# Projection in two passes over batch 0, and the first head's stack over two rings

## The chip, the cores and the metric

The kernel runs on one core of a Trainium2 chip. A core has five engines that work side by side and meet at semaphores: TensorE (PE, matmuls into PSUM), VectorE (DVE), ScalarE (ACT), GpSimd (POOL) and SyncE (SP, which here only issues DMAs). DMAs can be issued from SP, ACT and POOL; each of the three has a ring of its own. The metric is the device time of one launch in microseconds (us), lower is better; several runs are taken and the median is given.

## The reference

One transformer block on x, two batches of 2048 rows of 256 features. What matters here is its first part:

```
h = layernorm(x) * (1 + ca) + sa
Q, K, V = h @ W.T + b + 2 * (h @ A.T @ B.T)       # for Wq, Wk, Wv: 256 x 256, rank 8
energy = Q K^T / 4                                # 16 heads of 16 features, per batch
out = softmax(energy) V                           # 2048 keys and 2048 queries per head
x = x + ga * (out @ Wo.T + ...)                   # then a gated feed-forward stage with 8 experts
```

sa, ca, ga come from a small matrix product with wmod. There are 2 x 16 = 32 (batch, head) pairs, called heads below. The output projection, the shared and the routed feed-forward stages follow; neither they nor the arithmetic of any step is touched.

## The kernel before

**Chunks.** x is cut into 8 chunks of 512 rows (NCH), 4 per batch (CPB). For each chunk DVE takes mean and variance (`moments`), ACT a square root (`root`), DVE normalizes (`normalize`), PE transposes the result into PSUM (`turn`), ACT applies scale and shift and writes hT (`modulate`). PE then makes four units `qk` (o = 0 and 1: the first and second 128 columns of Q; o = 2 and 3: the same of K) and two halves of V (`v`). Heads 0 to 7 of a batch live in units 0 and 2, so head 0 needs only those.

**Parts.** Each unit is cut into three bf16 parts whose sum is the fp32 value: ACT writes a copy and the first part (`take`), POOL the remainder, ACT the middle part (`middle`), POOL the last part; SP stores the three (384 KB) to DRAM as qk_parts (`store`). `take` and `middle` of ACT, and the two POOL steps, are in a written order, one engine instruction after the other.

**Stacks.** Before a head can run, `stack` reads its rows of Q and K parts back from DRAM into four tiles: q_high and k_high (64 KB and 128 KB a DMA, 8 DMAs), q_low and k_low. All 16 DMAs are issued by SP, in SP's order. There are three sets of tiles; the first three heads' stacks are issued during the projection. k_low also has rows of ones, and q_low has two rows that hold each query's negated maximum; those come from POOL tiles `mb` by four small DMAs of SP (`maxima`) once the head's maxima are known.

**Maxima.** For each head PE makes 32 pairs of matmuls k_high x q_high (`max_pair`, L847), and DVE takes a maximum of each (`reduce_pair`, L937). A pair needs two banks of a ring of three PSUM banks, so a pair directly behind a pair waits for DVE. Head 0's 32 pairs stand between the units of batch 1, as the table BESIDE says: 2 in chunk 4, then 8, 11 and 11. Behind them stand 12 pairs of head 1, mixed with four products for rowmod (L915), then the first scores of head 0 (`scores`, L870), which wait for head 0's two maximum rows through s_mrows. After that the 32 heads run in a steady rhythm.

**SP's order.** Loads; then per chunk of batch 0 the next x load and four stores; a wait for all of them; stack of head 0; chunk 4's stores; stack of head 1; four small late loads; chunk 5's stores; stack of head 2; three weight loads of 512 KB; the stores of chunks 6 and 7; then `maxima` of heads 0 and 1.

**Buffers.** Two tiles for x, two for the normalized x, two for hT, four for parts. POOL first fills rows of ones in three k_low tiles and clears three vs tiles, and then begins with the remainders.

Of the kernel before, what the change touches and what calls it, by code (L numbers as in the profile page):

```python
# [26 lines left out]
F32 = mybir.dt.float32  # L27
# [6 lines left out]
P = 128  # L34
# [29 lines left out]
STACK = 16 * 16  # L64
UQ = 2 * D // P
TAGS = 4
# [82 lines left out]
def block_kernel(nc, io, out):  # L149
    with ExitStack() as ctx:  # L150
# [72 lines left out]
        x_t = buffers("x_t", [P, TPC, D], F32, r)  # L223
        xn = buffers("xn", [P, TPC, D], F32, r)
        hT = buffers("hT", [P, HALF, CH], F32, r)
        qf = buffers("qf", [P, CH], F32, r, UQ)
        parts = buffers("parts", [P, 3, CH], BF16, r, UQ)
        stats = r("stats", [P, TPC, 6])
        mv = r("mv", [P, TPC, 2])
        std = r("std", [P, TPC])  # L230

        turned_sb = Region(nc, r.at, queries_at)("turned_sb", [KT, P])
# [3 lines left out]
        rest = buffers("rest", [P, CH], F32, r, UQ)  # L236
        loA = r("loA", [R, 4, D])
        loB = r("loB", [R, 4, D])

# [67 lines left out]
        s_wT = sem("s_wT")  # L307
        s_wmod = sem("s_wmod")
# [13 lines left out]
        s_x = [sem(f"s_xload{u}") for u in range(2)]  # L322
# [10 lines left out]
        s_parts = [sem(f"s_parts{o}") for o in range(UQ)]  # L333
# [3 lines left out]
        s_stack = [sem(f"s_stack{p}") for p in range(NB)]  # L337
        s_rows = sem("s_rows")
# [80 lines left out]
        def root(act, g):  # L419

            act.wait_ge(s_var, g + 1)
            act.activation(std[:], mv[:, :, 1], ACT.Sqrt, bias=eps[:, 0:1]).then_inc(s_std, 1)

        def moments(dve, step, g, u, nth):

            dve.wait_ge(s_x[u], 16 * (nth + 1))
            for t in range(TPC):
                st = dve.bn_stats(stats[:, t, :], x_t[u][:, t, :])
            step(st)
            hold(dve)  # L430
            for t in range(TPC):
                a = dve.bn_aggr(mv[:, t, :], stats[:, t, :])
            a.then_inc(s_var, 1)

        def normalize(dve, step, g, u):

            dve.wait_ge(s_std, g + 1)
            step(dve.reciprocal(std[:], std[:]))
            wait(dve, s_xn_free, g - 1)
            for t in range(TPC):  # L440
                a = dve.tensor_scalar(xn[u][:, t, :], x_t[u][:, t, :], mv[:, t, 0:1], std[:, t:t + 1],
                                      ALU.subtract, ALU.mult)
            a.then_inc(s_norm, 1)


        def setup_sync(sp):

            for dst, src in first_loads[:-1]:
                sp.dma_start(dst[:], src).then_inc(s_const, 16)
            sp.dma_start(wT[:], io["wT"]).then_inc(s_wT, 16)  # L450
            sp.dma_start(x_t[1][:], rows(io["x"], TPC, TPC)).then_inc(s_x[1], 16)
            dst, src = first_loads[-1]
            sp.dma_start(dst[:], src).then_inc(s_bv, 16)
            sp.wait_ge(s_norm, 1)
            sp.dma_start(x_t[0][:], rows(io["x"], 2 * TPC, TPC)).then_inc(s_x[0], 16)
            sp.dma_start(wmod[:, :, 512:], io["wmod"][:, :, 512:]).then_inc(s_wrow, 16)

        def setup_scalar(act):
            act.dma_start(x_t[0][:], rows(io["x"], 0, TPC)).then_inc(s_x[0], 16)
# [7 lines left out]
        def setup_tensor(pe):  # L467
            pe.wait_ge(s_const, 16 * (len(first_loads) - 1))
            for m in range(4):
# [3 lines left out]
            mm.then_inc(s_lora, 1)  # L473
            pe.wait_ge(s_wmod, 16)
# [5 lines left out]
            mm.then_inc(s_mcol, 1)  # L480

        def setup_vector(dve, step):
            step(dve.memset(eps[:], EPS))
# [3 lines left out]
            moments(dve, step, 0, 0, 0)  # L487
            normalize(dve, step, 0, 0)
# [4 lines left out]
            dve.wait_ge(s_lora, 1)  # L493
            for m in range(4):
                dst = wqkv[:, m] if m < 3 else woT[:]
                w = dve.scalar_tensor_tensor(dst.rearrange("p k d -> p (k d)"), ps[:, 4 + m, :], LORA_SCALE,
                                             wT[:, m].rearrange("p k d -> p (k d)"), ALU.mult, ALU.add)
            w.then_inc(s_weff, 1)
# [3 lines left out]
            moments(dve, step, 1, 1, 0)  # L502
            normalize(dve, step, 1, 1)
# [21 lines left out]
        def project_sync(sp):  # L525
            def load(g, u):
                sp.dma_start(x_t[u][:], rows(io["x"], g * TPC, TPC)).then_inc(s_x[u], 16)

            def store(g, b, j):

                for o in range(UQ):
                    half = o % 2
                    sp.wait_ge(s_qf_free, UQ + UQ * g + o + 1)
                    dst = qk_dram[o // 2].rearrange("s (b c) t -> c s b t", b=B)
                    sp.dma_start(dst[half * P:(half + 1) * P, :, bass.ds(b, 1), bass.ds(j * CH, CH)].squeeze(2),
                                 parts[o][:]).then_inc(s_parts[o], 16)
# [7 lines left out]
            sp.wait_ge(s_norm, NCH - 2)  # L544
            load(NCH - 1, 1)
            for o in range(UQ):
                sp.wait_ge(s_parts[o], 16 * (CPB + 1))
# [10 lines left out]
            for g in range(CPB + 2, NCH):  # L558
                store(g, 1, g % CPB)


        BESIDE = {CPB: 2, CPB + 1: 8, CPB + 2: 11, CPB + 3: PAIRS - 21}

        def units_beside(g):

            if g not in BESIDE:
                return iter(()), [0] * 7
            first = sum(n for c, n in BESIDE.items() if c < g)
            n = BESIDE[g]
            share = [0, 0, 0, 0, 0, 0, n] if g == CPB else [n * (i + 1) // 7 - n * i // 7 for i in range(7)]  # L570
            return iter(range(first, first + n)), share

        def project_tensor(pe):
            pe.sem_inc(s_v, 1)

            def turn(g, u):
                pe.wait_ge(s_norm, g + 1)
                wait(pe, s_hT, g)
                for k in range(HALF):
                    for t in range(TPC):  # L580
                        mm = pe.transpose(ps[:, k, t * P:(t + 1) * P], xn[u][:, t, k * P:(k + 1) * P], ident[:])
                mm.then_inc(s_xn_free, 1)

            def qk(g, u, o):
                pe.wait_ge(s_qbank_free, UQ * g + o + 1)
                for k in range(HALF):
                    mm = pe.matmul(ps[:, 2 + o % 2, :], wqkv[:, o // 2, k, (o % 2) * P:(o % 2 + 1) * P],  # L587
                                   hT[u][:, k, :], start=(k == 0), stop=(k == 1))
                mm.then_inc(s_unit, 1)

            def v(g, u, half):
# [1234 lines left out]
```

## Time and profile before

| what | us |
|---|---|
| median of 3 runs | 1972.77 |
| lowest and highest | 1971.50, 1974.07 |
| the profiled execution: its own time | 1975.94 |
| its span in the trace | 1974.1 |
| mean granted TensorE clock in it | 0.973 of full speed |

In the span PE is busy 1864.3 us (94%), DVE 1559.0, ACT 1245.7 and POOL 341.5. The span has three stretches. The projection and the lead into attention take the first 180 us, the 32 heads run from there to about 1480 us (some 40 us a head), and the rest is the output projection and the feed-forward part. A row of the timeline gives the start, the busy time of the group, engine, line, operation, tiles and count, and in brackets the idle time before it with what ended it. A fp32 matmul of the code is shown as two instructions in the trace. For an instruction that issues a DMA the time is that of the issue, not of the transfer.

### The profile page before, as it was taken

What the parts mean: (1) busy time and instruction counts of PE and PEld (TensorE: products, weight loads), DVE (VectorE), ACT (ScalarE), POOL (GpSimd) and SP (SyncE); (2) the same over time, 40 slices, a digit from 0 to 9 for tenths busy, and PEclk for the clock granted to TensorE, in tenths of its full rate; (3) what the DMA queues carried; (4) which work ended last, traced back from release to release, by engine and by line L of the source; (5) the groups of instructions that cost most, each with busy time, mean ns of one, the idle gap of its engine ahead of it and who ended that gap; (6) DMA issues with size and microseconds to landing.
All of it is one profiled execution on the core that took longest, in us unless ns stands there. A gap on an engine that the chain in (4) does not pass through costs nothing.

```text
span 1974.1 us, 34939 instructions
## 1 busy us (share of the span) xinstructions
PE 1864.3 (94%) x13114; PEld 770.4 (39%) x13115; DVE 1559.0 (79%) x2738; ACT 1245.7 (63%) x1426; POOL 341.5 (17%) x425
## 2 busy tenths in 40 slices
PE   7687999999999999999999999999984799999997
PEld 5332222222222222222222222222224556589996
DVE  5376999999999999999999999999816732245553
ACT  4534777777777777777777777777871221144442
POOL 6534200000000000000000000000015622223332
PEclk9898999999999999999999999999997799999998
DMA  4541111211112111111112111111047432322221
GB/s 160 167 149 37 42 41 39 61 57 43 41 46 68 46 41 41 58 59 42 41 48 65 49 38 39 57 56 41 7 143 227 164 102 91 117 81 73 72 72 48
DMA packets 89737, 141.52 MB, mean 72 GB/s; under 512 B 13104, under 2 KB 60208, under 8 KB 89472
## 3 DMA queue, kind: packets, MB, share of 16 engines
q1 hardware_dynamic: 74336, 102.01, 16.5%
q0 software_dynamic: 10240, 32.40, 5.0%
q10 hardware_dynamic: 5024, 5.24, 0.8%
q8 instruction: 91, 1.49, 0.3%
q14 instruction: 46, 0.38, 0.1%
HBM read 90.84 MB, written 48.51 MB: 71 GB/s over the span
## 4 chain that ended last, share of the span: by engine, by line
PE 81%; DVE 9%; DMA 3%; POOL 2%; issue 2%; ACT 1%; SPq 1%; POOLq 0%; DVEq 0%; ACTq 0%
PE ps L881 24%; PE ps L870 20%; PE ps L847 15%; PE ps L1560 7%; DVE mx L937 6%; PE ps L1111 5%; PE ps L1583 3%; PE ps L1445 3%; DMA l_in<-inverse_sums 2%; PE ps L587 1%; ACT prob L962 1%; POOL parts L727 1%; POOL rest L723 1%; PE ps L915 1%; PE ps L596 1%
## 5 line engine op out<-in xcount | busy, mean ns | idle before, releaser
L937 DVE TENSOR_REDUCE mx<-ps 128x1 f32<-128x512 f32 x2048 | 1273.3, 683 | 58.7 <-PE ps L847 55.5
L962 ACT ACTIVATE prob<-ps 128x1024 f32<-128x1024 f32 x1024 | 992.4, 1021 | 275.1 <-PE ps L870 272.6
L881 PE MATMUL ps<-prob,vs 128*32 128x512 f32 x4096 | 546.5, 605 | 0.7 <-ACT prob L962 0.7
L847 PE MATMUL ps<-k_high,q_high 64*128 64x512 bf16 x2048 | 400.8, 388 | 33.3 <-DMA k_low<-qk_parts 16.8
L870 PE MATMUL ps<-q_high,k_high 64*128 64x512 bf16 x2048 | 389.8, 377 | 3.3 <-ACT prob L962 2.2
L870 PE MATMUL ps<-q_low,k_low 34*128 34x512 bf16 x2048 | 390.0, 377 | 0.0
L847 PEld LDWEIGHTS ps<-k_high,q_high 64*128 64x128 bf16 x2048 | 99.1, 93 | 668.4 <-DVE mx L937 628.1
L1016 POOL CAST mb<-turned_sb 16x128 bf16<-16x128 f32 x32 | 8.9, 279 | 925.3 <-ACT turned_sb L975 896.9
L870 PEld LDWEIGHTS ps<-q_low,k_low 34*128 34x128 bf16 x2048 | 100.0, 94 | 116.9 <-issue 0.5
L870 PEld LDWEIGHTS ps<-q_high,k_high 64*128 64x128 bf16 x2048 | 101.5, 96 | 88.7 <-ACT prob L962 30.0
L881 PEld LDWEIGHTS ps<-prob,vs 128*32 128x32 f32 x4096 | 80.7, 108 | 118.7 <-issue 113.4
L1646 DVE TENSOR_TENSOR ehT<-esig,ps 128x512 f32<-128x512 f32 x39 | 26.8, 688 | 100.6 <-PE ps L1560 100.6
L1466 ACT ACTIVATE sgate<-ps 128x512 f32<-128x512 f32 x32 | 19.1, 597 | 121.6 <-PE ps L1111 121.6
L1607 ACT ACTIVATE esig<-ps 128x512 f32<-128x512 f32 x39 | 23.3, 597 | 113.4 <-PE ps L1560 113.4
L1319 DVE TENSOR_TENSOR hid<-sgate,ps 128x512 f32<-128x512 f32 x32 | 22.0, 687 | 76.5 <-ACT sgate L1466 76.5
L1560 PE MATMUL ps<-xsT,gate_w 128*128 128x128 f32 x624 | 76.1, 275 | 1.6 <-issue 1.0
L1560 PEld LDWEIGHTS ps<-xsT,gate_w 128*128 128x128 f32 x624 | 75.6, 192 | 3.9 <-issue 1.2
L1560 PE MATMUL ps<-xsT,up_w 128*128 128x128 f32 x624 | 76.1, 275 | 0.0
L1583 PE MATMUL ps<-rdT,ehT 128*128 x312 | 73.6, 379 | 0.0
L1560 PEld LDWEIGHTS ps<-xsT,up_w 128*128 128x128 f32 x624 | 72.8, 192 | 0.0
L1136 PE MATMUL ps<-woT,o_in 128*128 128x256 f32 x128 | 38.5, 469 | 33.2 <-DVE o_in L1187 33.2
L1111 PE MATMUL ps<-h2T,wgT 128*128 (+1 forms) x128 | 64.0, 625 | 4.4 <-DVE x L1197 4.1
(146 smaller groups left out, 1416.4 us busy)
## 6 DMA issues: line engine op xcount, KB each, us to landing
k_high<-qk_parts SPq DMA_DIRECT2D x128, 128.0 KB
qk_parts<-parts SPq DMA_DIRECT2D x32, 384.0 KB, 3.8
q_high<-qk_parts SPq DMA_DIRECT2D x128, 64.0 KB
k_low<-qk_parts SPq DMA_DIRECT2D x128, 64.0 KB
head_out<-head_out_sb SPq DMA_DIRECT2D x32, 256.0 KB, 10.8
sorted_in<-zero_row POOLq DMA_DIRECT2D x13, 390.0 KB, 7.3
xs<-sorted_in SPq DMA_DIRECT2D x39, 130.0 KB
q_low<-qk_parts SPq DMA_DIRECT2D x128, 32.0 KB
```

The source lines that it names most:

```text
L847: pe.matmul(ps[:, ring.bank((n, m, u)), :], q_high[p][mine, t * P:(t + 1) * P], k_high[p][mine, c * CH:(c + 1) * CH], start=True, stop=Tru ...
L870: mm = pe.matmul(ps[:, 2 * i + u, :], keys[mine, kt * P:(kt + 1) * P], queries[mine, i * CH:(i + 1) * CH], start=(n == 0), stop=(n == 1))
L881: mm = pe.matmul(ps[32 * j:32 * j + 32, 7, :], vs[buf(h)][:, kt, :], prob[:, kt % 2, j * CH:(j + 1) * CH], start=(kt == 0), stop=(kt == KT ...
L937: dve.tensor_reduce(mx[n % 2][:, at, c:c + 1], ps[:, ring.bank(what), :], AX.X, ALU.max).then_inc(s_ring, 1)
L962: act.activation(prob[:, kt % 2, :].rearrange("p (u c n) -> p u c n", u=2, c=2)[:, :, half, :], ps[:, 2 * half:2 * half + 2, :], ACT.Exp). ...
L1111: mm = pe.matmul(ps[:, at, :], w[:, k, fc * P:(fc + 1) * P], h2T[:, k, bass.ds(g * CH, CH)], start=(k == 0), stop=(k == 1))
L1136: mm = pe.matmul(ps[:, OUT_BANK[u] + t // 2, t % 2 * D:(t % 2 + 1) * D], o_in[u][:, k, t * P:(t + 1) * P], woT[:, k, :], start=(k == 0), s ...
L1445: mm = pe.matmul(ps[:, DOWN_BANK[u] + t // 2, t % 2 * D:(t % 2 + 1) * D], hid[u][:, fc, t * P:(t + 1) * P], wdT[:, fc, :], start=(fc == 0) ...
L1560: mm = pe.matmul(ps[:, bank, fc * P:(fc + 1) * P], w[u][:, c, fc * P:(fc + 1) * P], xsT[u][:, c, :], start=(c == 0), stop=(c == 1))
L1583: mm = pe.matmul(ps[:, 6 + u, 0:D], ehT[u][:, c, :], rdT[:, bass.ds(e, 1), c, :].squeeze(1), start=(c == 0), stop=(c == FC - 1))
L1607: act.activation(esig[u][:].rearrange("p c n -> p (c n)"), ps[:, egate_bank(k), :], ACT.Silu).then_inc(s_esig, 1)
L1646: dve.tensor_tensor(ehT[u][:].rearrange("p c n -> p (c n)"), esig[u][:].rearrange("p c n -> p (c n)"), ps[:, eup_bank(k), :], ALU.mult).th ...
```

## The change

Batch 0 is projected in two passes. The first makes units 0 and 2 of chunks 0 to 3 (eight units, EARLY), whose stores are all that head 0's stack needs. The second makes units 1 and 3 and V. hT of all four chunks stays in four tiles. The stack of head 0 goes out between the passes: its high tiles' first halves from SP, the second halves from POOL. Of the other DMAs of the stacks of heads 0 and 1, a few each stand between SP's stores; head 2's stack is issued behind the last store of chunk 7. `stack` now issues the eight high DMAs first, then six for the low tiles: q_low is read by one DMA per half in the place of two (64 KB, shaped 2 x 16 rows). The low tiles are counted with s_mrows.

x has eight tiles (four of them in the upper half of v_all, free until batch 1's V), all requested at once, normalized in place. The adapters and effective weights of Q and K are made before those of V and O. POOL's fills of ones wait for the second chunk's normalization, its clears of vs go behind the first pass. Parts have six tiles. Head 0's pairs stand 8 in chunk 3's second pass, in twos, and 6 in each chunk of batch 1, one behind each unit or half of V. The loops over chunks are written out.

**PE, from the adapters to the first pairs.** Before (the loop body over batch 0 stands once, and runs twice):

```order
L471 MATMUL ps<-loB,loA 128x256 x8
L478 MATMUL ps<-cS,wmod 128x2 x8
L581 MATMUL ps<-ident,xn_100 128x128 x8
...
L587 MATMUL ps<-hT_102,wqkv 128x512 x4
L596 MATMUL ps<-wqkv,hT_102 128x256 x4
L587 MATMUL ps<-hT_102,wqkv 128x512 x4
L596 MATMUL ps<-wqkv,hT_102 128x256 x4
L847 MATMUL ps<-k_high_66,q_high_81 128x512 x4
L581 MATMUL ps<-ident,xn_100 128x128 x8
```

After, from the first pass's end:

```order
L619 MATMUL ps<-hT_126,wqkv 128x512 x4
L619 MATMUL ps<-hT_127,wqkv 128x512 x4
L619 MATMUL ps<-hT_102,wqkv 128x512 x2
L628 MATMUL ps<-wqkv,hT_102 128x256 x4
...
L619 MATMUL ps<-hT_126,wqkv 128x512 x2
L628 MATMUL ps<-wqkv,hT_126 128x256 x4
L505 MATMUL ps<-ident,x_t_98 128x128 x8
L619 MATMUL ps<-hT_127,wqkv 128x512 x2
L909 MATMUL ps<-k_high_66,q_high_81 128x512 x4
```

The first pair stood behind the whole of chunk 4; it now stands behind the first pass, three chunks of the second pass (the dots), a transposition and one unit.

**SP, around the stack of head 2** (q_high_83 and k_high_68). Before, the stack stands behind chunk 5's stores, and the stores of chunks 6 and 7 behind it:

```order
L535 DMA qk_parts<-parts_111 128x3x512
L780 DMA q_high_83<-qk_parts 32x1x1024
L781 DMA k_high_68<-qk_parts 32x1x2048
...
L557 DMA wdT<-in_wdT 128x1024
L535 DMA qk_parts<-parts_108 128x3x512
...
L798 DMA q_low_84<-mb_73 1x8x128 x4
```

After:

```order
L581 DMA qk_parts<-parts_109 128x3x512
L829 DMA q_high_83<-qk_parts 32x1x1024
L830 DMA k_high_68<-qk_parts 32x1x2048
...
L610 DMA wdT<-in_wdT 128x1024
L858 DMA q_low_84<-mb_73 1x8x128 x4
```

The stack and the three weight loads now stand between the last store and the four DMAs for head 0's maximum rows (q_low from mb).

**POOL, at the end of the first pass,** after:

```order
L774 TENSOR_TENSOR parts_109<-rest_123,parts_109 128x512
L783 MEMSET vs_64 128x512
L784 MEMSET vs_64 128x16
...
L769 TENSOR_TENSOR rest_120<-qf_104,parts_110 128x512
L829 DMA q_high_81<-qk_parts 32x1x1024
L830 DMA k_high_66<-qk_parts 32x1x2048
L829 DMA q_high_81<-qk_parts 32x1x1024
L830 DMA k_high_66<-qk_parts 32x1x2048
L769 TENSOR_TENSOR rest_121<-qf_105,parts_111 128x512
```

POOL issued no DMA in the projection before; four now stand among its remainders, behind a wait for the first pass's stores.

The core of the diff:

```diff
 def project_sync(sp):
-    with sp.Fori(0, CPB // 2) as i:
-        for u in range(2):
-            g = 2 * i + u
-            sp.wait_ge(s_norm, g + 2)
-            load(g + 3, 1 - u)
-            store(g, 0, g)
...
-    stack(sp, (0, 0))
-    store(CPB, 1, 0)
-    stack(sp, (0, 1))
+    for g in range(CPB):
+        store(g, 0, 2)
+    parts_stored(sp, EARLY)
+    stack_high(sp, (0, 0), 0)
+    store(0, 1)
+    sp.dma_start(wmod[:, :, 512:], io["wmod"][:, :, 512:]).then_inc(s_wrow, 16)
+    store(0, 3)
+    sp.wait_ge(s_rows, 1)
+    stack_low(sp, (0, 0), 0)
+    store(1, 1)
+    stack_low(sp, (0, 0), 1)
+    store(1, 3)
+    stack_high(sp, (0, 1), 0)
...
-    store(CPB + 1, 1, 1)
+    for g in range(CPB, NCH):
+        store(g, *range(UQ))
     stack(sp, (0, 2))
     for dst, name in ((wgT, "wgT"), (wuT, "wuT"), (wdT, "wdT")):
         sp.dma_start(dst[:], io[name]).then_inc(s_shared, 16)
-    for g in range(CPB + 2, NCH):
-        store(g, 1, g % CPB)
 def project_tensor(pe):
+    pe.wait_ge(s_weff, 1)
+    for g in range(CPB):
+        if g + 1 < CPB:
+            turn_chunk(pe, g + 1)
+        pe.wait_ge(s_hT, g + 1)
+        qk(g, 0)
+        qk(g, 2)
+    pe.wait_ge(s_weff, 2)
+    for g in range(CPB - 1):
+        qk(g, 1)
+        v(g, 0)
+        qk(g, 3)
+        v(g, 1)
...
+            qk(g, 2 * i)
+            max_pair(pe, (0, 0), first)
+            qk(g, 2 * i + 1)
+            max_pair(pe, (0, 0), first + 1)
+            v(g, i)
+            max_pair(pe, (0, 0), first + 2)
 def project_gpsimd(pool, step):
+    pool.sem_inc(s_qf_free, UQ)
+    pool.wait_ge(s_norm, 2)
...
+    remainder(EARLY)
+    parts_stored(pool, EARLY)
+    stack_high(pool, (0, 0), 1, s_stack_first)
+    for n in range(EARLY + 1, UQ * NCH):
+        remainder(n)
+        last_part(n - 1)
+def stack_low(eng, h, u):
+    p, q_parts, k_parts = buf(h), qk_dram[0], qk_dram[1]
+    mine, first = slice(num(h) * DH, (num(h) + 1) * DH), u * HROWS
+    eng.dma_start(q_low[p][first:first + LROWS, :], q_parts[0:3:2, mine, u * HS:(u + 1) * HS]
+                  ).then_inc(s_mrows[p], 16)
```

## Rows read from the trace of the kernel before

**Rows 1.** PE's timeline, the start: start us, busy us, line, operation, tiles.

```profile
7.43 7.19 PE L471 MATMUL ps<-loB,loA 8*128 8x256 f32 x16 [7.43 <-DMA bqk_in<-in_bqk]
14.54 3.57 PE L478 MATMUL ps<-cS,wmod 128*128 128x2 f32 x16
17.98 1.95 PE L581 MATMUL ps<-ident,xn 128*128 128x128 f32 x8
...
24.21 4.09 PE L587 MATMUL ps<-hT,wqkv 128*128 128x512 f32 x8
```

**Rows 2.** A chunk of batch 0 on PE, and the wait behind batch 0.

```profile
35.03 1.04 PE L581 MATMUL ps<-ident,xn 128*128 128x128 f32 x8
35.90 3.60 PE L587 MATMUL ps<-hT,wqkv 128*128 128x512 f32 x8
39.34 1.89 PE L596 MATMUL ps<-wqkv,hT 128*128 128x256 f32 x8
41.07 3.60 PE L587 MATMUL ps<-hT,wqkv 128*128 128x512 f32 x8
...
96.82 0.61 PE L847 MATMUL ps<-k_high,q_high 64*128 64x512 bf16 x2 [16.84 <-DMA k_low<-qk_parts]
```

**Rows 3.** Batch 1 with head 0's pairs on PE, same view.

```profile
106.58 0.39 PE L847 MATMUL ps<-k_high,q_high 64*128 64x512 bf16 x2
...
108.83 0.39 PE L847 MATMUL ps<-k_high,q_high 64*128 64x512 bf16 x2
...
121.76 0.39 PE L847 MATMUL ps<-k_high,q_high 64*128 64x512 bf16 x2 [0.78 <-DVE mx L937]
...
127.69 0.39 PE L847 MATMUL ps<-k_high,q_high 64*128 64x512 bf16 x2 [1.06 <-DVE mx L937]
...
158.20 0.53 PE L847 MATMUL ps<-k_high,q_high 64*128 64x512 bf16 x2 [0.90 <-DVE mx L937]
```

**Rows 4.** The first scores of head 0 on PE, timeline of all engines.

```profile
180.71 0.38 PE L870 MATMUL ps<-q_high,k_high 64*128 64x512 bf16 x2
```

**Rows 5.** One chunk of batch 0 on ACT, from the timeline.

```profile
20.83 1.45 ACT L635 ACTIVATE hT<-ps,colmod 128x512 f32<-128x512 f32 x2
...
26.63 0.69 ACT L643 ACTIVATE qf<-ps,bqk 128x512 f32<-128x512 f32 x1 [0.63 <-PE ps L587]
...
29.50 0.62 ACT L650 CAST parts<-rest 128x512 bf16<-128x512 f32 x1
```

**Rows 6.** First normalization on DVE, beside POOL's fills.

```profile
9.39 4.81 DVE L441 TENSOR_SCALAR xn<-x_t,mv,std 128x256 f32<-128x256 f32 x4
```

**Rows 7.** POOL in the projection, from the timeline.

```profile
0.74 3.65 POOL L715 MEMSET k_low<- 2x2048 bf16 x2 [0.29 <-POOLq L1816]
...
30.81 1.15 POOL L727 TENSOR_TENSOR parts<-rest,parts 128x512 bf16<-128x512 f32 x1
```

**Rows 8.** SP in the projection, from the timeline: DMA issues.

```profile
76.57 0.78 SPq L780 DMA_DIRECT2D q_high<-qk_parts  x1
...
118.57 0.64 SPq L780 DMA_DIRECT2D q_high<-qk_parts  x1
...
130.76 0.43 SPq L557 DMA_DIRECT2D wdT<-in_wdT  x1
```

**Rows 9.** DMAs up to 150 us: KB each, median us to landing.

```profile
qk_parts<-parts SPq DMA_DIRECT2D x28, 384.0 KB, 3.9
...
k_high<-qk_parts SPq DMA_DIRECT2D x12, 128.0 KB
...
wdT<-in_wdT SPq DMA_DIRECT2D x1, 512.0 KB, 15.3
```

**Rows 10.** One us of attention; last three: granted clock, DMA share, GB/s.

```profile
1088.00:1089.00 1.00, 1.00 (x14) 0.29 (x12) 1.00 (x2) 0.67 (x1) 0.00 (x0) 1.00 0.13 51
```

**Rows 11.** A steady head's timeline: SP's first stack DMA, DVE's mneg.

```profile
1030.86 0.68 SPq L780 DMA_DIRECT2D q_high<-qk_parts  x1
...
1062.32 0.21 DVE L944 TENSOR_REDUCE mneg<-mx 128x16 f32<-128x64 f32 x1
```

More of the change, by code:

```diff
@@ L320, in block_kernel @@
         s_gates = sem("s_gates")
-        s_x = [sem(f"s_xload{u}") for u in range(2)]
+        s_x = [sem(f"s_xload{g}") for g in range(NCH)]
         s_var = sem("s_var")
@@ L465, in setup_scalar, with unit, adapt @@
             root(act, 1)
-        def setup_tensor(pe):
-            pe.wait_ge(s_const, 16 * (len(first_loads) - 1))
-            for m in range(4):
+        def unit(g, o):
+            return 2 * g + o // 2 if g < CPB and o % 2 == 0 else EARLY + 2 * g + o // 2 if g < CPB else UQ * g + o
+        def adapt(pe, first):
+            for m in range(first, first + 2):
                 for k in range(HALF):
@@ L492, in setup_vector @@
             dve.wait_ge(s_wT, 16)
[L493 to L498, printed above, removed]
+            effective(0)
+            moments(dve, step, 1)
             dve.wait_ge(s_mcol, 1)
@@ L557, in project_sync, with qk, v @@
                 sp.dma_start(dst[:], io[name]).then_inc(s_shared, 16)
-            for g in range(CPB + 2, NCH):
-                store(g, 1, g % CPB)
[L562 to L571, printed above, removed]
         def project_tensor(pe):
             pe.sem_inc(s_v, 1)
-            def turn(g, u):
-                pe.wait_ge(s_norm, g + 1)
-                wait(pe, s_hT, g)
+            def qk(g, o):
+                n = unit(g, o)
+                pe.wait_ge(s_qbank_free, n + 1)
                 for k in range(HALF):
[L580 to L588, printed above, removed]
+                    mm = pe.matmul(ps[:, 2 + n % 2, :], wqkv[:, o // 2, k, (o % 2) * P:(o % 2 + 1) * P],
+                                   hT[g % CPB][:, k, :], start=(k == 0), stop=(k == 1))
                 mm.then_inc(s_unit, 1)
-            def v(g, u, half):
+            def v(g, half):
                 pe.wait_ge(s_vbank_free, 2 * g + half + 1)
@@ L667, in project_scalar @@
-            modulate(0, 0, 0)
-            with act.Fori(0, CPB // 2) as i:
-                for u in range(2):
-                    chunk(2 * i + u, u, (2 * i + u + 1) // CPB, True, True)
-            for g in range(CPB, NCH):
-                chunk(g, g % 2, 1, g + 1 < NCH, g + 2 < NCH)
+                n = unit(g, o)
+                slot, bank, scale = n % UQ, 2 + n % 2, 0.25 if o < 2 else 1.0
+                act.wait_ge(s_unit, n + 1)
+                act.wait_ge(s_qf_free, n + 1)
+                act.activation(qf[slot][:], ps[:, bank, :], ACT.Identity, bias=bqk[:, o:o + 1], scale=scale)
@@ new lines, in take, with middle @@
+                act.wait_ge(s_parts[n % SLOTS], 16 * (n // SLOTS + 1))
+                act.activation(parts[n % SLOTS][:, 0, :], ps[:, bank, :], ACT.Identity, bias=bqk[:, o:o + 1],
+                               scale=scale).then_inc(s_qbank_free, 1)
+            def middle(n):
+                act.wait_ge(s_rest, n + 1)
+                act.copy(parts[n % SLOTS][:, 1, :], rest[n % UQ][:]).then_inc(s_mid, 1)
+            modulate(0)
+            for g in range(CPB):
+                if not g:
+                    root(act, 2)
+                if g + 1 < CPB:
+                    modulate(g + 1)
+                take(g, 0)
+                if g:
+                    middle(2 * g - 1)
+                else:
+                    root(act, 3)
+                take(g, 2)
+                middle(2 * g)
```

321 lines of the change are left out of this document (175 added, 146 removed).

## The prediction

> **What bounds the kernel now.** I read three views. The timeline of PE comes first, since PE is busy for 94% of the span. In batch 0 PE runs chunk after chunk with no gap worth the name: a transposition 0.87 us (35.03 to 35.90), two units 3.44, a half of V 1.73, so 11.2 us a chunk [rows 2]. Then it stands for 16.84 us until the last DMA of head 0's stack has landed, at 96.82 [rows 2]. In batch 1 a unit or half of V with one pair behind it takes 2.25 us (106.58 to 108.83); a pair directly behind a pair adds 0.78 or 1.06 of waiting for DVE and its own 0.39 [rows 3]. The projection ends at 158.20 with head 1's first pair [rows 3], head 0's first scores stand at 180.71 [rows 4]. Second, SP's issues: the first stack starts at 76.57, the third at 118.57, and the weight loads behind that one end with wdT, issued at 130.76 [rows 8]. Third, the DMA views: a store lands in 3.9 us, wdT in 15.3 [rows 9], and in a stretch in which almost only a stack is moving the DMA share is 0.13 of 16 engines at 51 GB/s [rows 10]. 0.13 x 16 is two engines busy and fourteen idle. A stack's eight high DMAs are four of 128 KB and four of 64 KB, 786 kB in all, 15.4 us at that rate; the first stack took 20.2 us from first issue to landing (76.57 to 96.82), so some 3.8 us are start, low tiles and landing.
>
> Behind 180 us the change reaches only the order in which a stack's DMAs are issued, so I sum the start and check the rest under the rivals.
>
> **The start.** PE's chain is now: half of the adapters (7.43 + 3.56), the wmod product (3.44), a transposition at the early pace (1.95), the other half (3.56), another transposition (1.95): 21.9 for the first unit against 24.21 [rows 1]. DVE's first normalization took 4.81 beside POOL's fills [rows 6]; with the fills moved away it is shorter, but PE waits for neither, since its own chain is longer. The x loads are all requested early; x of chunk 1 is needed when DVE has made the weights of Q and K, about 12.4 us, and nothing here waited for a later x. Gain 2.3.
>
> **Pass one.** PE alone would need 8 units of 1.72 and two transpositions, 15.5 us. It won't get them. POOL's fills of ones are 3 x 3.65 = 11 us [rows 7] and start at the second normalization, about 16.7, so POOL is free at 27.8 and the first remainder, 1.15 [rows 7], is done at 28.9. ACT's order puts its cast (0.6) and then hT of chunk 2 (1.45) behind it [rows 5]: 31.0. Then come two takes of 1.2 and two casts, 3.7, and hT of chunk 3: 36.1. Unit 8 of the pass needs the bank of unit 6, whose take ends after take, cast, take, at 39.0; unit 8 ends at 40.8. So 3.4 us are lost against PE alone. POOL, from 27.8 on with 16 operations of 1.12 to 1.15 and about 1.7 of waiting for ACT, has the last part at 47.5. Its store lands at 51.5 [rows 9].
>
> **Pass two, and the stack under it.** Three chunks of two units and two halves of V are 3 x 6.9 = 20.7, the transposition 0.87, one unit 1.9: the first pair stands at 64.3. The stack is issued from 51.6. If the rings work side by side, each moves 393 kB: 7.7 us, with the 3.8 of before 63.1, so 1.2 us ahead of PE. If they share two engines it is 15.4 + 3.8 = 70.8, and PE waits 6.5. Below, a landing cannot beat a store's 3.9 us, and even that would give PE nothing more. I take the first case, because the row shows fourteen engines idle: two rings have room to be on different ones [rows 10]. POOL's order holds a wait for the stores and four issues, about 0.7 us each at SP's price [rows 8]; behind them stand the remainders that ACT needs for its take of pass two's fourth to sixth units. POOL resumes at about 54.5, that take ends at 58, and PE comes for that bank at 58.2: nothing is lost, and 1 us would be if an issue cost 1 us.
>
> On whether two rings help, the row shows two engines busy. The Trainium skill, page "DMA: Bandwidth & Descriptors", section "Issuing engines are not separate DMA queues", says that issuing from several engines saves only the sequencer's time, as all run on the same 16 engines; by that alone the wait would be 6.5. Its section "Why a DMA increments its semaphore by 16 and not by 1" says that a copy whose outermost dimension is 2 runs on two engines, for SP and ACT the lowest two, for POOL the next ones of a rotating cursor, which would make it 0. The trace agrees with the two engines; no run here shows POOL's.
>
> **Chunk 3 and batch 1.** Chunk 3 is four steps of 2.25, two second pairs behind a unit (1.17) and two behind V (1.45): 14.2. From the transposition's end at 62.4 that is 76.6. Batch 1 is 24 steps of 2.25 and three transpositions of 1.04: 57.1, and 0.9 before the next pair [rows 3]: head 1's first pair at 134.6. DVE has three pairs and one eviction in 6.7 us there and keeps up, and ACT and POOL have some 2.3 us of work for a unit that comes every 3.6. Stores are held up behind the stacks of heads 0 and 1 on the two engines, by up to 8 us each time, and six tiles of parts cover about 20. Against 158.20 this is 23.6 us earlier: 16.8 for the wait, about 5 for fewer pairs directly behind pairs, the 2.3 of the start, about 3 for the slow restart behind the wait (the pair at 96.82 took 0.61, later ones 0.39), less 3.4 of pass one.
>
> **The tail.** From head 1's first pair to the first scores are 22.5 us of pairs and rowmod products (158.20 to 180.71), and those stay. But the first scores also need head 0's maximum rows, four DMAs of 2 KB. Before, SP's ring was empty when they were issued. Now they stand behind stack 2 and three loads of 512 KB. The last unit ends 3.5 us ahead of the pair, its last part 4.4 us later, so the stack is issued 1.3 us behind that pair. In the trace of before stack and loads took from 118.57 to 130.76 + 15.3 = 146.1, 27.5 us [rows 8, 9]; that gives 28.8. q_low is now shaped like the high copies, and at 51 GB/s its two DMAs are 2.6 us: 31. Summed up from the rates (15.4 + 2.6 for the two engines, 4 to 5 for the loads and k_low, 3.8 less 1 for the rest) it is 28. I take 29: rows at 29, wanted at 22.5, a new wait of 6.5. It can't be below 0, and above it is 10.
>
> **The sum.** 23.6 - 6.5 = 17.1. The profiled execution took 1975.94 with a span of 1974.1; its span becomes 1957.0. The median of the runs is 1972.77, 3.2 below that execution, and I take the same difference off it: 1955.7.
>
> **The rivals.**
> 1. *The two rings share engines.* The wait at the first pair is 6.5 instead of 0. For it: before, all DMAs of a stack used two engines, one after the other. Against it: the other ring. It decides once the stack lands after 64.3, and I leave only 1.2 us, so a late POOL or a slow store would do it in part. 1962.2.
> 2. *The maximum rows are not held up* (other engines, or the loads pass them). For it: small DMAs. Against it: wdT's 15.3 us. The tail costs 0: 1949.2.
> 3. *Slower.* In attention the stack is shaped anew for every head: high first, q_low on two engines. Its place is the next head's first pair, some 30 us behind the stack's first issue (1030.86 to just ahead of 1062.32) [rows 11]; the high DMAs need 19. The rows of the head in between go out behind the stack's end at 25. If either came late by more than 0.6 us a head, 30 heads would eat up the 17. There are 5 to 10 us of room, so little speaks for it: from 1974 on, say 1990.
> 4. *The change doesn't do what it says:* pass one's chain through ACT, POOL and the store is so late that PE still stands 10 us or more for the stack, beside the wait in the tail. For it: POOL's late start. Against it: the sum above. With 14 us, 1970.
>
> **The numbers.** Forecast 0.47, rival 1 0.25, rival 2 0.17, rival 4 0.05, rival 3 0.03, and 0.03 for an unseen loss. The forecast's own range is 1952 to 1960; eight times in ten the time should lie between 1948 (rival 2 with a start a little better) and 1965 (rival 1 with a longer tail). About 0.2%, 4 us, is what can be told from no change: faster 0.93, same 0.03, slower 0.04.
>
> **What would show it.** PE's first unit near 22 and pass one's end near 41. POOL's last part of pass one near 47.5. PE's idle time before head 0's first pair: 0 to 1 right, 5 or more rival 1. Head 1's first pair near 135. PE's idle time before the first scores, put down to a DMA into q_low: 5 to 8 right, none rival 2. The period of a head unchanged at about 40 us, else rival 3. I would be wrong above all if ACT or POOL held PE in pass two, or if stores arrived so late that ACT's takes ran out of parts tiles.

## The result: 0.2% faster where 0.9% was forecast

| what | before | after |
|---|---|---|
| median of 20 runs each | 1974.07 us | 1970.69 us |
| lowest and highest | 1971.07, 1978.07 | 1966.30, 1972.81 |
| span of the profiled execution | 1974.1 us | 1969.9 us |
| mean granted TensorE clock in it | 0.973 | 0.976 |

The ratio of the times is 0.9982, with a 95% interval of 0.9975 to 0.9989. The change is faster, by 3.4 us and not by 17, and the time lies more than 5 us above the wider range of the prediction (1948 to 1965). The first scores tell the same as the whole: they stand at 176.27 against 180.71 [rows 4], 4.4 earlier, and the span is 4.2 shorter. So all of the shortfall lies ahead of 176 us.

PE's timeline of the changed kernel up to the first scores. The columns are those of [rows 1]:

```profile
21.95 4.91 PE L619 MATMUL ps<-hT,wqkv 128*128 128x512 f32 x8
...
37.65 5.39 PE L619 MATMUL ps<-hT,wqkv 128*128 128x512 f32 x12 [1.02 <-ACT parts L688]
...
58.88 1.88 PE L619 MATMUL ps<-hT,wqkv 128*128 128x512 f32 x4
67.65 3.78 PE L628 MATMUL ps<-wqkv,hT 128*128 128x256 f32 x8 [6.89 <-DVE v_all L731]
71.23 1.59 PE L505 MATMUL ps<-ident,x_t 128*128 128x128 f32 x8
...
74.47 0.39 PE L909 MATMUL ps<-k_high,q_high 64*128 64x512 bf16 x2
...
144.22 0.39 PE L909 MATMUL ps<-k_high,q_high 64*128 64x512 bf16 x2 [1.15 <-DVE mx L999]
...
163.38 0.39 PE L909 MATMUL ps<-k_high,q_high 64*128 64x512 bf16 x2 [0.80 <-DVE mx L999]
176.27 0.61 PE L932 MATMUL ps<-q_high,k_high 64*128 64x512 bf16 x2 [12.50 <-issue]
```

The first unit stands at 21.95 (24.21 before [rows 1]) and head 0's first pair at 74.47 (96.82 [rows 2]), with no wait directly ahead of it. That looks like success until one reads the row in front: PE stood for 6.89 us at 67.65, put down to DVE's eviction of V (L731), of which the prediction said nothing. From head 0's first pair to head 1's first pair are 69.75 us. Then there is a wait of 12.50 ahead of the first scores.

Why DVE was late with V, on DVE's timeline of the changed kernel:

```profile
50.23 2.28 DVE L451 TENSOR_SCALAR x_t<-x_t,mv,std 128x256 f32<-128x256 f32 x4
...
56.45 10.55 DVE L451 TENSOR_SCALAR x_t<-x_t,mv,std 128x256 f32<-128x256 f32 x4
66.92 0.68 DVE L731 TENSOR_TENSOR v_all<-ps,bv_row 128x512 f32<-128x512 f32 x1
```

The same line asked for alone between 56 and 67 us (durations in ns, least, median and most):

```profile
L451 DVE TENSOR_SCALAR x_t<-x_t,mv,std x4: 402/403/9579, 56.4 to 66.6; 128x256 f32<-128x256 f32 x4
```

One of the four instructions that normalize chunk 6 took 9579 ns, and the others about 400. The same four for chunk 5, 6 us earlier, took 2.28 together. POOL in the same stretch:

```profile
54.69 1.23 POOL L769 TENSOR_TENSOR rest<-qf,parts 128x512 f32<-128x512 f32 x1
55.80 1.23 POOL L774 TENSOR_TENSOR parts<-rest,parts 128x512 bf16<-128x512 f32 x1
...
64.70 1.17 POOL L774 TENSOR_TENSOR parts<-rest,parts 128x512 bf16<-128x512 f32 x1
```

From 54.69 on POOL ran ten operations with no gap between them, one every 1.11 us, and stopped at 65.87. DVE's long instruction, the first of the four, ended at about 66.0 (56.45 + 9.58).

PE's stop also cost clock. Stretches of the changed kernel (length, busy time and count of PE, PEld, DVE, ACT and POOL, then granted clock, DMA share, GB/s):

```profile
66.00:68.00 2.00, 0.35 (x1) 0.35 (x2) 1.60 (x5) 0.00 (x0) 0.00 (x0) 0.50 0.67 215
68.00:72.00 4.00, 4.00 (x12) 3.15 (x12) 0.53 (x1) 0.00 (x0) 0.00 (x0) 0.50 0.27 96
...
170.00:175.00 5.00, 0.00 (x0) 0.00 (x0) 0.00 (x0) 0.00 (x0) 1.13 (x1) 0.50 0.13 51
```

Behind the wait the half of V took 3.78 us and not 1.89, and the transposition 1.59 and not 1.04, at a granted clock of 0.50: 2.4 us more. So the late V is worth 6.89 + 2.4 = 9.3 us.

SP, from which the other wait came:

```profile
51.42 0.75 SPq L829 DMA_DIRECT2D q_high<-qk_parts  x1
...
145.69 0.61 SPq L829 DMA_DIRECT2D q_high<-qk_parts  x1
...
160.61 1.85 SPq L610 DMA_DIRECT2D wdT<-in_wdT  x1
162.71 3.44 SPq L858 DMA_DIRECT2D q_low<-mb  x4
```

The profile puts the 12.50 down to "issue", that is, to nothing that it shows, so the cause had to be looked for. Head 2's stack starts at 145.69, and head 0's maximum rows (L858) are issued 17 us behind that. They are used at 176.27, and in the last microseconds before it (170 to 175 above) the DMA engines run as in [rows 10]: share 0.13, 51 GB/s. So it looks as if the rows come behind the stack; the experiments test that.

### The profile page after: what moved, and what is told of

It reads as the page before. It is cut to its first block, busy times and chain, and to the rows that moved or that the text cites. A ratio compares the mean times of both kernels' runs of the same rounds, so it can differ in the third digit from the quotient of the medians.

```text
span 1969.9 us, 34636 instructions
## 1 busy us (share of the span) xinstructions
PE 1867.0 (95%) x13114; PEld 769.8 (39%) x13115; DVE 1570.3 (80%) x2738; ACT 1244.8 (63%) x1423; POOL 344.1 (17%) x429
## 4 chain that ended last, share of the span: by engine, by line
PE 83%; DVE 10%; DMA 2%; ACT 2%; issue 2%; POOL 1%; SPq 1%; POOLq 0%; DVEq 0%; ACTq 0%
PE ps L943 24%; PE ps L932 20%; PE ps L909 15%; PE ps L1621 7%; DVE mx L999 6%; PE ps L1172 5%; PE ps L1644 3%; PE ps L1506 3%; PE ps L619 2%; DMA l_in<-inverse_sums 2%; PE ps L628 1%; ACT prob L1024 1%; DVE x_t L451 1%; DVE x L1258 1%; PE ps L977 0%
## 5 line engine op out<-in xcount | busy, mean ns | idle before, releaser
L932 PE MATMUL ps<-q_high,k_high 64*128 64x512 bf16 x2048 | 390.2, 378 | 15.4 <-issue 12.5
L1668 ACT ACTIVATE esig<-ps 128x512 f32<-128x512 f32 x39 | 23.3, 597 | 113.4 <-PE ps L1621 113.4
L1172 PE MATMUL ps<-h2T,wgT 128*128 (+1 forms) x128 | 64.1, 625 | 4.6 <-DVE x L1258 4.4
```

What stands on the lines that cost most here:

```text
L932: mm = pe.matmul(ps[:, 2 * i + u, :], keys[mine, kt * P:(kt + 1) * P], queries[mine, i * CH:(i + 1) * CH], start=(n == 0), stop=(n == 1))
L1172: mm = pe.matmul(ps[:, at, :], w[:, k, fc * P:(fc + 1) * P], h2T[:, k, bass.ds(g * CH, CH)], start=(k == 0), stop=(k == 1))
```

## The experiments

Times are medians; each ratio is to the kernel before, run beside it on the same chip, with its 95% interval. The kernel before had medians from 1972.98 to 1974.55 there, so a difference between the medians of two experiments can be off by 2 or 3 us; the ratios are the better measure where that matters. Where a kernel is built on another experiment, the text says so.

### Is it the normalization? norm_later

DVE's order, chunks 6 and 7 moved from pass two into chunks 4 and 5 of batch 1:

```diff
-                normalize(dve, step, CPB + g + 1)
+                if g == 0:
+                    normalize(dve, step, CPB + 1)
...
                     v(g, i)
+                    if i == 0 and g < CPB + 2:
+                        normalize(dve, step, g + 2)
```

> The changed kernel with one edit: DVE's normalizations of chunks 6 and 7 leave pass two (where POOL runs without a gap) and stand in chunks 4 and 5 of batch 1. Theory (a TENSOR_SCALAR of DVE stood for 9.6 us because POOL gave it no gap): it now takes under 1 us an instruction, PE does not stop at about 60.6, head 0's first pair stands at 64 to 66 instead of 74.5, and the kernel is 9 to 10 us faster than the changed one, about 1961. Rival (the four DVE instructions were slow because of the DMA traffic of stack, wmod and stores): the V halves of chunk 2 are then free too, but the instructions are slow where they now stand, if the traffic is as dense. Rival (both rings use the same two DMA engines): PE waits up to 6.5 us at the first pair instead, which then stands at 71.

Measured: 1963.53 us, ratio 0.9941 (0.9926 to 0.9956), span 1961.4. PE:

```profile
65.62 0.39 PE L912 MATMUL ps<-k_high,q_high 64*128 64x512 bf16 x2 [0.57 <-DMA k_high<-qk_parts]
...
167.31 0.61 PE L935 MATMUL ps<-q_high,k_high 64*128 64x512 bf16 x2 [12.60 <-issue]
```

The first pair is 8.9 us earlier, the span 8.5 shorter and the median 7.2 lower, where 9 to 10 was expected, and the tail's wait is what it was. The first failed step is DVE's normalization in pass two.

### POOL's stream, or what it reads? thin_pool and pool_pause

thin_pool leaves part of the computation out: POOL's last parts of pass two's units are made for 16 columns of 512.

```diff
-                pool.tensor_tensor(parts[n % SLOTS][:, 2, :], rest[n % UQ][:], parts[n % SLOTS][:, 1, :],
+                w = 16 if EARLY <= n < 2 * EARLY else CH
+                pool.tensor_tensor(parts[n % SLOTS][:, 2, 0:w], rest[n % UQ][:, 0:w], parts[n % SLOTS][:, 1, 0:w],
```

> The changed kernel in its own order, but POOL's last parts of pass two (units 8 to 15) are made for 16 of 512 columns only; the other columns of those third parts are left out. All DMAs move the same bytes. POOL's duty falls to about half, with gaps between its remainders. Theory (POOL's unbroken stream holds DVE off): no TENSOR_SCALAR over 2.5 us in pass two, PE not stopped for V, first pair at 64 to 66. Rival (DMA traffic holds DVE off): the instruction of 9.6 us stays, first pair at 74.

Measured: one execution, 1965.21 us, span 1963.2. DVE and PE of it:

```profile
56.46 2.78 DVE L451 TENSOR_SCALAR x_t<-x_t,mv,std 128x256 f32<-128x256 f32 x4
...
66.59 0.39 PE L910 MATMUL ps<-k_high,q_high 64*128 64x512 bf16 x2 [1.49 <-DMA k_high<-qk_parts]
```

The normalization stands where it stood, beside the same stores and the same stack, and takes 2.78 and not 10.55. So DMA traffic is not what held it. This kernel also has less work on POOL, so a second one keeps all of it and only makes POOL stop once:

```diff
             for n in range(EARLY + 1, UQ * NCH):
+                if n == EARLY + 2:
+                    pool.wait_ge(s_norm, CPB + 3)
                 remainder(n)
```

> The changed kernel with one wait added on POOL: ahead of the remainder of the pass-two unit that it comes to at about 56.9 us, POOL stands still until chunk 6 is normalized. All work is still done, the stores and stacks are the same. My theory (POOL's operations, one directly behind the other, keep DVE's x_t instruction out until they pause): the normalization that took 10.55 us from 56.45 takes 1.6 to 2.8; POOL stops for about 1.3 to 2 us and its stream ends near 67.5 instead of 65.9; head 0's first pair stands at 65 to 67 instead of 74.5; chunk 7's normalization, which follows at about 63.4, may be held until about 67, which costs the pairs 1 us or 2. Span 1961 to 1964. Rival (the instruction was slow for what it reads or for DMA traffic, and the order of POOL's work doesn't matter): it still takes about 10 us, and the pause makes POOL later by as much; first pair at 74 or later, span 1970 to 1980.

Measured: 1963.18 us, ratio 0.9956 (0.9942 to 0.9970), span 1961.2. POOL, then DVE, of this kernel:

```profile
55.60 1.23 POOL L774 TENSOR_TENSOR parts<-rest,parts 128x512 bf16<-128x512 f32 x1
58.05 1.15 POOL L769 TENSOR_TENSOR rest<-qf,parts 128x512 f32<-128x512 f32 x1 [1.21 <-DVE x_t L451]
...
62.50 1.16 POOL L769 TENSOR_TENSOR rest<-qf,parts 128x512 f32<-128x512 f32 x1
63.62 1.21 POOL L774 TENSOR_TENSOR parts<-rest,parts 128x512 bf16<-128x512 f32 x1
64.79 1.20 POOL L769 TENSOR_TENSOR rest<-qf,parts 128x512 f32<-128x512 f32 x1
65.95 1.20 POOL L774 TENSOR_TENSOR parts<-rest,parts 128x512 bf16<-128x512 f32 x1
```

```profile
56.26 1.71 DVE L451 TENSOR_SCALAR x_t<-x_t,mv,std 128x256 f32<-128x256 f32 x4
63.15 4.15 DVE L451 TENSOR_SCALAR x_t<-x_t,mv,std 128x256 f32<-128x256 f32 x4
```

A pause of 1.21 us on POOL makes DVE's 10.55 us into 1.71, and a kernel with one wait more is 7.5 us faster than the changed one by the medians, 5 by the ratios and 8.7 by the spans. That settles the cause: in the changed kernel DVE's instruction got no turn until POOL stopped, and a pause gives it one. It does not follow that a stream without a pause always holds DVE off. The second DVE row is chunk 7's normalization. It ran beside a POOL stream without a gap too, and its four instructions ended one by one:

```profile
L451 DVE TENSOR_SCALAR x_t<-x_t,mv,std x4: 668/1240/1244, 63.1 to 66.1; 128x256 f32<-128x256 f32 x4
```

So there DVE got one instruction in per POOL operation (1.24 us each), and in the changed kernel none in eight operations. The pace of POOL is not what tells the two apart: DVE's first instruction came in at 63.15, beside an operation that the next one followed after 1.12 us (62.50 to 63.62), as in the changed kernel, and only from 63.62 on do they come every 1.16. The wider pace begins with DVE's turns. What the rows do show is that the operations that held DVE off are recorded as 1.17 to 1.23 us long, so that each overlaps the next by 0.07 to 0.12, and the one at 62.50 as 1.16, with an overlap of 0.04. Whether that decides it, no run tested, and why the one stream let DVE in and the other didn't stays open.

The Trainium skill, page "SBUF — State Buffer", section "Who interferes with whom", says that VectorE and GpSimd share a pair of ports, that a tensor_scalar on VectorE can take it, and that the one that comes second waits fully until the first one's instruction is over. The 1.24 us an instruction agree with it. The 9.58 us don't: by that rule an instruction would wait for one operation of 1.2, and here it waited for eight.

### The tail: tail_as_before, both

SP's order as before the change: stack 2 and the loads behind chunk 5's stores.

```diff
-            for g in range(CPB, NCH):
+            for g in range(CPB, CPB + 2):
                 store(g, *range(UQ))
             stack(sp, (0, 2))
...
+            for g in range(CPB + 2, NCH):
+                store(g, *range(UQ))
```

> The changed kernel with SP's end of the projection as before: the third stack and the three 512 KB loads stand behind chunk 5's stores, chunks 6 and 7's stores behind them. Theory (the maximum rows of head 0 queue behind that stack and those loads): the 12.5 us of idle PE before the first scores are gone, the scores stand at about 164 instead of 176.3, the kernel is 11 to 13 us faster than the changed one, about 1958. Rival (the rows are late for another reason, POOL's or SP's own work): the wait stays above 5 us. Rival (stores held up by the stack reach ACT and PE in chunks 6 and 7): a part of the gain comes back as idle PE there.

Measured: 1972.69 us, ratio 0.9985 (0.9973 to 0.9997), span 1969.0: nothing gained. SP and PE:

```profile
138.72 20.65 SPq L581 DMA_DIRECT2D qk_parts<-parts  x8
```

```profile
155.03 0.61 PE L911 MATMUL ps<-k_high,q_high 64*128 64x512 bf16 x2 [11.97 <-ACT parts L690]
```

The wait ahead of the scores is gone, and one of 11.97 stands ahead of head 1's first pair. The eight stores of chunks 6 and 7 are issued behind the stack, from 138.72 on, ACT runs out of parts tiles, and PE out of banks. That is the last rival, and it took all of the gain and not a part. In the kernel before the same order cost PE nothing, because its projection ended later: the stores went out from 131.24 on, 27 us ahead of head 1's first pair (158.20 [rows 3]), and here only 4 us ahead of where that pair would have stood without the wait. With the normalizations moved as well:

> Both edits. Theory: they are independent, one ahead of head 0's first pair and one behind the last, so the gains add up to 21 to 23 us over the changed kernel: 1948 to 1950. Rival: one uncovers the other's wait (stack not landed at the first pair, or stores late), and less than 18 us are left.

Measured: 1964.2 us, ratio 0.9943 (0.9926 to 0.9960), span 1964.0, with 12.06 in the same place, so less than 18 us are left, as the rival said. The stack costs 12 us on either side of those stores; its place among them is not the lever.

### What the rows wait for: rows_first, loads_last, rows_on_act

All three stand on norm_later (1963.53). rows_first puts `stack(sp, (0, 2))` and the three loads behind SP's `maxima((0, 0))`; loads_last does so with the loads alone. rows_on_act takes `maxima((0, 0))` from SP and lets ACT issue the same four DMAs between its products for rowmod:

```diff
+                if c == 1:
+                    act.wait_ge(s_mb, 1)
+                    for u in range(2):
+                        for m in range(2):
+                            row = u * HROWS + LROWS + m
+                            act.dma_start(q_low[0][row:row + 1, :].rearrange("a (t c) -> a t c", t=HT),
+                                          mb[0][u * HT:(u + 1) * HT, m, :]).then_inc(s_mrows[0], 16)
```

> Base: the kernel with DVE's normalizations of chunks 6 and 7 moved (norm_later, 1963.5, 12.6 us of idle PE before the first scores). Edit: SP issues head 0's maximum rows first, then the third stack and the three loads, then head 1's rows. Theory (the rows only queue behind them): the idle time before the first scores falls from 12.6 to 0 or 1, scores at 155 instead of 167.3, 11 to 13 us faster: 1951 to 1952.5. Head 2's first pair is 27 us behind the scores and its high tiles need 19, so nothing new waits. Rival (a stack in flight always costs somebody some 12 us, as in tail_as_before, where the stores took the wait over): a wait of 5 us or more shows at head 2's first pair or in head 1's rows.

> Base norm_later. Edit: only the three 512 KB loads go behind head 0's rows; the third stack stays ahead of them. Theory: of the 12.6 us the loads are 4 to 5 (1.5 MB over sixteen engines, 98 kB each behind the stack on the two busy ones) and the stack the rest: 8 us of idle PE are left, 4 to 5 us faster than the base, 1959. Rival (the loads alone block the row DMAs, since they fill the ring last): the wait goes to 0.

> Base norm_later. Edit: ACT issues head 0's four row DMAs on its own ring, behind its second copy of rowmod; SP's order is unchanged. Theory A (the rows wait in SP's ring, in ring order): on another ring they land within 5 us although the same DMA engines are busy with the stack, idle PE before the scores 0 to 1, 1951 to 1953. Theory B (they wait for the two busy DMA engines whatever ring they are on): they land with the stack, 8 us or more of idle PE, 1959 or slower.

| kernel | us | ratio | span | PE's wait ahead of the first scores |
|---|---|---|---|---|
| norm_later | 1963.53 | 0.9941 (0.9926 to 0.9956) | 1961.4 | 12.60 |
| loads_last | 1958.86 | 0.9920 (0.9903 to 0.9937) | 1956.7 | 10.05 |
| rows_first | 1950.48 | 0.9874 (0.9855 to 0.9892) | 1949.2 | none |
| rows_on_act | 1947.40 | 0.9860 (0.9844 to 0.9877) | 1946.4 | none |

In loads_last the scores come 27.96 us behind head 1's first pair (135.46 to 163.42), against 31.95 in norm_later (135.36 to 167.31): the loads are 4.0 of it, the stack the rest. The time is what was expected. The wait is 10.05 and not 8, because the pairs and products ahead of the scores took only 17.9 us (135.46 to 153.36) at a granted clock of 1.00; in norm_later they took 19.4, at 0.91. In rows_first the scores stand at 155.73, and PE waits nowhere for more than 2.03 us from there to head 2's first pairs, so the stack's 12 us did not move on to another place. In rows_on_act SP's stack starts at its old place and is still being issued when the rows go out and are used. SP, ACT and PE of that kernel:

```profile
136.81 0.62 SPq L832 DMA_DIRECT2D q_high<-qk_parts  x1
...
148.04 2.59 SPq L844 DMA_DIRECT2D k_low<-qk_parts  x2
```

```profile
141.39 3.23 ACTq L1052 DMA_DIRECT2D q_low<-mb  x4
```

```profile
154.78 0.38 PE L934 MATMUL ps<-q_high,k_high 64*128 64x512 bf16 x2
```

The first scores stand 19.4 behind head 1's first pair (135.34), and 31.95 in norm_later, with the stack issued 1.5 behind that pair in both. The rows pass the stack. They had waited for their turn in SP's ring, not for DMA engines: at a DMA share of 0.13 fourteen engines were idle, and that didn't help four DMAs that stood behind the stack in the same ring.

To see whether the two failed steps add up, the ACT edit was also made on the changed kernel alone:

> The changed kernel with one edit: ACT issues the four row DMAs of head 0's maxima in the place of SP; nothing is moved on DVE. It separates the two failed steps. If they add up (the late pairs cost 7 to 8 us, SP's ring in the tail 12.5 and the work behind it some 3 more, as with the normalizations moved), the time is 16 us under the changed kernel's: 1954 to 1956, with the first pair still at 74.5 and no wait of PE ahead of the first scores. If the tail's wait only hid behind the late pairs, it would be nearer to 1960 or above.

Measured: 1958.84 us, ratio 0.9933 (0.9917 to 0.9950), span 1955.9. PE:

```profile
67.61 3.78 PE L628 MATMUL ps<-wqkv,hT 128*128 128x256 f32 x8 [6.89 <-DVE v_all L731]
...
163.53 0.38 PE L931 MATMUL ps<-q_high,k_high 64*128 64x512 bf16 x2
```

The first scores stand 12.7 us earlier than in the changed kernel, 9.0 earlier in norm_later (167.31), and 21.5 earlier with both edits (154.78): they add up in the traces (21.7). The spans say the same, 14.0, 8.5 and 23.5. The medians don't settle it: by them the two edits are worth 11.9 and 7.2, which leaves 4.2 of 23.3, and this median is 3 us above what was expected, between the two cases that the expectation set apart.

### Do two rings help? one_ring

On norm_later; SP issues both halves of head 0's high tiles.

```diff
             stack_high(sp, (0, 0), 0)
+            stack_high(sp, (0, 0), 1, s_stack_first)
...
-            stack_high(pool, (0, 0), 1, s_stack_first)
```

> Base norm_later. Edit: SP issues both halves of head 0's high tiles, POOL none. Theory (the eight high DMAs share two DMA engines when they are on one ring, 15.4 us, and different ones on two rings, where PE waited 0.6): the first pair comes 7 to 8 us later, PE idle 7 to 8 us, the kernel 7 to 8 us slower than the base, 1971, less up to 1 us for POOL's freed time. Rival (the two rings share engines anyway): no difference beyond SP's four issues, 0 to 2 us.

Measured: 1968.87 us, ratio 0.9975 (0.9965 to 0.9985), span 1965.0. PE, and one stretch of the stack of this kernel and then of norm_later:

```profile
71.73 0.61 PE L912 MATMUL ps<-k_high,q_high 64*128 64x512 bf16 x2 [5.47 <-DMA k_high<-qk_parts]
```

```profile
56.00:58.00 2.00, 2.00 (x8) 1.21 (x7) 0.69 (x1) 0.00 (x0) 2.00 (x3) 1.00 0.13 51
```

```profile
54.00:56.00 2.00, 2.00 (x10) 1.58 (x9) 0.39 (x1) 0.04 (x1) 2.00 (x4) 1.00 0.48 67
```

On one ring the stack takes 20.3 us from its first issue (51.44) to the pair that waits for it (71.73), like the 20.2 of before [rows 2, 8]. On two it takes 14.2 (51.42 to 65.62). From 54 to 56, before SP issues anything but the stack, the DMA share is 0.48 with two rings, seven or eight engines, and 0.13 on one ring, two engines; from 56 to 58 two rings move 139 GB/s and one ring 51. So the second ring's DMAs ran on other engines. The 5.47 us of waiting and the 5.3 us between the medians are rival 1, measured; the expectation had 7 to 8. The run also shows the first failed step once more, and mildly. POOL issues no DMAs here, so its remainders run beside chunk 5's normalization, which takes 3.96 us and not 2.28, and PE waits 0.98 us for V at 54.79:

```profile
50.17 3.96 DVE L451 TENSOR_SCALAR x_t<-x_t,mv,std 128x256 f32<-128x256 f32 x4
```

The Trainium skill, page "DMA: Bandwidth & Descriptors", section "Issuing engines are not separate DMA queues", would have given nothing for it beyond issue time; for DMAs that each use two engines, this run measures otherwise.

### One more step on the fastest: fills_early

On rows_on_act: four of POOL's six fills of ones at the very start, two at their place.

```diff
-            pool.wait_ge(s_norm, 2)
             for p in range(NB):
+                if p == 2:
+                    pool.wait_ge(s_norm, 2)
                 for u in range(2):
```

> The fastest so far (normalizations moved to batch 1, rows issued by ACT; 1947.4, first pair 65.6) with four of POOL's six fills of ones at the very start, ahead of the first normalization at about 9.4, and only two behind the second normalization. POOL is then free at about 20.5 instead of 27.9. If pass one is held up by POOL's and ACT's late start, as its waits say (0.41 and 1.02 in its third group and more behind), it ends near 37.6 instead of 41.1, POOL's last part near 44.2 instead of 47.65, the stack lands 3.4 us earlier, and the whole is 3 us faster: 1943 to 1945. Rival (the first stack is bound by stores or by something later, or the fills hold DVE's first normalization): within 1 us of 1947.4 or slower.

Measured: 1947.65 us, ratio 0.9868 (0.9851 to 0.9884), span 1945.4. POOL's early fills, DVE's third normalization and PE's first pair:

```profile
0.82 7.37 POOL L768 MEMSET k_low<- 2x2048 bf16 x4 [0.37 <-POOLq L1887]
```

```profile
18.89 2.47 DVE L451 TENSOR_SCALAR v_all<-v_all,mv,std 128x256 f32<-128x256 f32 x4
```

```profile
63.39 0.39 PE L912 MATMUL ps<-k_high,q_high 64*128 64x512 bf16 x2 [0.33 <-DMA k_high<-qk_parts]
```

The pair is 2.2 us earlier than in rows_on_act (65.58), and not 3.4: the third normalization took 7.11 beside the fills and now takes 2.47, but POOL, free at 20.2, now waits 5.90 us for ACT's first parts, which wait for PE's first unit. The span is 1.0 shorter and the median doesn't show a gain, so this one is not told from no change; the rival's number came true. Both kernels beat the changed one by 23 us and the one before by 1.3 to 1.4%.

## Why the prediction was wrong, step by step

- **The start: right.** 21.9 forecast, 21.95 measured.
- **Pass one: right.** Its end was put at 40.8; the group at 37.65 holds its last two units and the first of pass two, 1.72 each, so it ends at 41.1. POOL's last part was put at 47.5 and ends at 47.65.
- **Two rings: right, but the margin of 1.2 us was a slip.** 20.2 less 15.4 is 4.8 and not 3.8, so the stack should have landed at 64.1, 0.2 us ahead of PE. In norm_later, where nothing else holds PE, it lands at 65.62, 0.57 behind. On one ring the same sum gives 71.8 (51.6 + 15.4 + 4.8), and in one_ring the pair stood at 71.73.
- **Pass two, "nothing is lost": the first step that failed.** The working followed PE, ACT and POOL and had POOL resume at 54.5 (54.69 in the trace). It gave DVE no term there, though its order has the normalizations of batch 1 between V's evictions there. The sign was in the rows: the first normalization took 4.81 beside POOL's fills [rows 6], and the start's paragraph used just that, for another place. Behind its four DMA issues POOL had fallen back and ran without a pause, one DVE instruction stood for 9.58 us, and PE lost 9.3 us to it. The first pair came 10.2 us late; the last 0.9 are 0.3 from pass one's end and small waits such as 0.24 us for V at 50.16. The prediction had named the place (it would be wrong above all if ACT or POOL held PE in pass two), but not the way through DVE.
- **Chunk 3 and batch 1: right.** 70.3 us from pair to pair forecast, 69.75 measured.
- **The tail: right mechanism, wrong size; the second failed step.** The rows stand behind stack 2 and the loads, as said. But the wait is 12.5 and not 6.5. Half of the error is the side that waits; it makes the wait longer and costs no time. The lead of 22.5 was taken from before [rows 3, 4], where three of the four rowmod products took over 3 us (the first 3.50, at a mean granted clock of 0.80 from 158 to 170); now only the last does, and the lead is 19.6 (144.22 to 163.8). The first product before, and then after:

```profile
158.66 3.50 PE L915 MATMUL ps<-wmod,cB 128*128 128x512 f32 x4
```

```profile
144.55 1.98 PE L977 MATMUL ps<-wmod,cB 128*128 128x512 f32 x4
```

  The other half is the landing, and that does cost time: the scores stand 32.05 behind the pair and not 29. The prediction had 31 from the times of the trace before and 28 from the rates, and took 29; the 31 was the better one. The sum from the rates gives 26.1 to 27.1 by its own terms, and 27.1 to 28.1 with 4.8 for 3.8. The loads are 4.0 us of the landing, as forecast (loads_last), so what is missing belongs to the stack and the rows. It wasn't separated further.
- **Attention: right.** The period of a head is 40.4 us in both kernels, so rival 3 has no share.

The sum by the same steps: 10.2 late at the first pair, 0.6 won back in batch 1, 3.05 late at the landing. That makes the scores 12.7 us later than forecast, and 17.1 less 12.7 is 4.4 us, the gain that was measured. The bet on two rings had gone well, if with a margin that a correct subtraction would have put at 0.2 us; the range was too narrow because it only covered the rivals and left the engine that none of them named at zero.

## What to carry to other kernels

When an edit closes the gaps of one engine, list what every other engine runs in that stretch, and look for any row in which such an instruction was already slow beside it: POOL's stream without a pause held a DVE normalization for as long as it lasted (9.58 us), though not every such stream did, and one wait of a microsecond in it bought that back. A small DMA that something waits for should not be queued behind bulk copies that use few DMA engines; issue it from another engine's ring or ahead of them. A lead read from a stretch at a lower granted clock is not fixed: the same pairs and products took 22.5 us before (0.77 of full speed), 19.6 in the changed kernel (0.91) and 17.9 in loads_last (1.00). And a remainder that several terms rest on, like the 3.8 here, is worth a second subtraction.

## What the runs showed of the hardware beyond that

- One DVE TENSOR_SCALAR of 128x256 took 9.58 us beside POOL TENSOR_TENSORs without a gap (one per 1.11 us), 1.24 in pool_pause and one_ring beside ones without a gap that made way for it (one per 1.16 to 1.17), about 1.97 beside POOL's fills (four in 7.11 us), and 0.40 alone.
- Two rings moved head 0's stack, whose high DMAs use two engines each, in 14.2 us, and one ring in 20.3.
- Four DMAs of 2 KB, issued from ACT's ring while SP was issuing a stack and 1.5 MB of loads, held nobody up; in SP's ring, behind them, they made PE wait 12.6 us.
